# Edge-term gathers moved from the counts into layer 0, the gate ahead of them, uint16 tables, in a graph network kernel

## The reference

```python
h = relu(layernorm(x)); x = x + L0(h)       # gin: (h + segment_sum(h[src], dst)) @ W1, relu, @ W2
h = relu(layernorm(x)); x = x + L1(h)       # attention over the edges
h = relu(layernorm(x)); x = x + L2(h)       # mean over the neighbours
h = relu(layernorm(x)); x = x + L3(h)       # weighted sum over the edges

# L1, per edge and for 8 heads
scores = einsum(q[src], k[tgt]) / sqrt(16) + edges @ We + be
cons   = sigmoid(relu(conservation_scores @ Wc1 + bc1) @ Wc2 + bc2)   # per node: the gate
scores = scores * cons[tgt] + relu(distances @ Wd1 + bd1) @ Wd2 + bd2
weights = softmax of scores over the edges of each tgt
```

## Time and profile before

| | us |
|---|---|
| median of 3 runs | 5038.48 |
| the runs | 5023.93, 5038.48, 5147.51 |
| span of the profiled execution | 5145.3 |
| PE busy in it | 3841.6 (75%) |
| DVE busy | 3822.7 (74%) |
| POOL busy | 2737.6 (53%) |
| ACT busy | 1550.3 (30%) |

### The profile page before, as it was taken

The page is one execution under the profiler, slowest core; times in us unless marked ns, Lnnn a source line. Parts: engine busy times, 40 slices in busy tenths (PEclk is TensorE's granted clock), DMA queues, the critical chain, the costliest instruction groups (busy, mean ns, idle before and its releaser), DMA issues. The chain is left out here.

```text
span 5145.3 us, 93266 instructions
## 1 busy us (share of the span) xinstructions
PE 3841.6 (75%) x26234; PEld 2720.9 (53%) x26235; DVE 3822.7 (74%) x6359; ACT 1550.3 (30%) x3023; POOL 2737.6 (53%) x2300
## 2 busy tenths in 40 slices
PE   4685555550199968888888888888886348889999
PEld 2443222220189835555555555555554248888888
DVE  3516999991299989999999999999996699970000
ACT  2372234560101130122333444445552430020000
POOL 3430199996732227777777777777776232210000
PEclk8799999995599989999999999999997569999999
DMA  9674423346155444454555666666665535568887
GB/s 168 175 234 111 97 100 126 159 175 198 66 193 209 163 140 106 120 146 142 157 165 169 184 184 188 193 196 197 205 204 159 186 113 200 200 213 300 298 297 254
DMA packets 594376, 912.02 MB, mean 177 GB/s; under 512 B 107452, under 2 KB 519442, under 8 KB 575022
## 3 DMA queue, kind: packets, MB, share of 16 engines
q1 hardware_dynamic: 413024, 521.23, 31.2%
q10 hardware_dynamic: 117359, 250.68, 13.4%
q0 software_dynamic: 63872, 138.75, 11.3%
HBM read 608.33 MB, written 311.94 MB: 179 GB/s over the span
## 5 line engine op out<-in xcount | busy, mean ns | idle before, releaser
L1964 POOL DMA_INDIRECT at_qg<-q_d,at_slot x1616 | 1601.2, 991 | 495.8 <-issue 492.2
L986 PE MATMUL bw_ps<-bw_mov,bw_sta 128*128 128x392 bf16 x7056 | 1590.0, 349 | 19.2 <-issue 7.2
L986 PEld LDWEIGHTS bw_ps<-bw_mov,bw_sta 128*128 128x128 bf16 x7056 | 640.4, 102 | 365.0 <-issue 95.6
L2007 PE MATMUL at_psk<-at_kp,at_hot 128*128 x4848 | 611.7, 234 | 286.8 <-DVE at_qg L2085 244.4
L1051 POOL DMA_INDIRECT tv_rows<-ed_d,tv_place x101 | 628.2, 6219 | 339.1 <-DMA edv_d<-tv_rows 211.0
L2007 PEld LDWEIGHTS at_psk<-at_kp,at_hot 128*128 128x128 bf16 x4848 | 439.1, 101 | 624.1 <-issue 418.1
L889 PE MATMUL ba_ps<-ba_mov,ba_sta 128*128 128x392 bf16 x1968 | 380.4, 338 | 352.6 <-DVE ba_sta L830 309.1
L874 DVE TENSOR_SCALAR ba_mov<-iota,key,scale 128x392 bf16<-128x392 f16 x1968 | 592.4, 365 | 2.8 <-PEq L853 2.8
L970 DVE TENSOR_TENSOR bw_sta<-bw_raw,kw 128x1024 bf16<-128x1024 bf16 x882 | 561.2, 689 | 0.0
L830 DVE TENSOR_TENSOR bw_mov<-bw_ps,lo 128x3136 bf16<-128x3136 f16 x294 | 523.4, 1780 | 7.6 <-PE bw_ps L986 5.4
L1566 PE MATMUL at_p3t<-tile,room 128*128 128x256 f32 (+1 forms) x2450 | 524.2, 376 | 4.6 <-ACT room L1150 4.6
(11 more groups left out here) (537 smaller groups left out, 4668.3 us busy)
## 6 DMA issues: line engine op xcount, KB each, us to landing
tile<-adw_d SPq DMA_DIRECT2D x23, 6272.0 KB, 18.7
adw_d<-xall ACTq DMA_DIRECT2D x65, 1568.0 KB
adj_d<-ba_stage ACTq DMA_DIRECT2D x50, 1568.0 KB, 5.1
l0raw<-adj_d SPq DMA_DIRECT2D x50, 1568.0 KB, 6.6
tile<-adj_d SPq DMA_DIRECT2D x50, 1568.0 KB, 6.5
adw_d<-bw_stage ACTq DMA_DIRECT2D x33, 1568.0 KB
at_rel<-rel_d SPq DMA_DIRECT2D x101, 512.0 KB
et_attr<-in_edge_attr SPq DMA_DIRECT2D x48, 1024.0 KB
```

Source lines behind the costliest of these rows:

```text
L986: ins = pe.matmul(self.ps[:, bass.DynSlice(place, WCOL)], self.sta[:, k, u // 2, :, u % 2], self.mov[:, u // 2, :, u % 2], start=False, st ...
L1964: pool.indirect_dma_start(out=qg[:, ring, b, :], out_offset=None, in_=q_d[:, :], in_offset=bass.IndirectOffsetOnAxis(ap=slot[:, ring, b:b ...
L2007: ins = pe.matmul(ps_k[:, at:at + KW], hot[:, par, sum(ROUNDS[:r]) + u, :], kp[:].rearrange("p j k n -> p (j k n)")[:, bass.DynSlice(place ...
```

## The change

Three edits.

1. `terms_by_visits` becomes the class `TermsByVisits` with a ring of two. Its gathers are issued by GpSimd in layer 0, two in each of the 50 steps behind the block's rows and own sums and one behind the last, and its stores by SP, two behind each load of a raw block from the third on. GpSimd's steps of layer 0 are written out where they were a loop. The places of the gathers are copied by VectorE at the start of layer 0.
2. The gate's inputs are loaded by SP ahead of the mask rows, on a semaphore of their own, and GpSimd computes the gate with nothing in front of it in the counts. SP waits for its store before the barrier.
3. The tables of window numbers and window ends are uint16 in memory and on the chip, with one more cast on VectorE for each of the two tables (`firstv_u`).

```diff
-def terms_by_visits(nc, c, ctx):
-
-    ve, pool, sp = nc.vector, nc.gpsimd, nc.sync
-    ring = 4
-    place = ctx.enter_context(nc.sbuf_tensor("tv_place", [P, NG2], I32))
-    rows = ctx.enter_context(nc.sbuf_tensor("tv_rows", [P, ring, 2 * P], F32))
-    s_got, s_kept = ([c.sem(f"tv_{n}{k}") for k in range(ring)] for n in ("got", "kept"))
-    m = c.V(ve.tensor_copy(place[:], c.index[:, :, UK]))
-    wait(pool, m)
-    for g in range(NG2):
-        k, lap = g % ring, g // ring
+class TermsByVisits:
+
+
+    def __init__(self, nc, c, sb):
+        self.nc, self.c, self.ring = nc, c, 2
+        self.place, self.rows = sb("place", [P, NG2], I32), sb("rows", [P, self.ring, 2 * P])
+        self.s_got, self.s_kept = ([c.sem(f"tv_{n}{k}") for k in range(self.ring)] for n in ("got", "kept"))
+
+    def places(self):
+        wait(self.nc.gpsimd, self.c.V(self.nc.vector.tensor_copy(self.place[:], self.c.index[:, :, UK])))
+
+    def gather(self, g):
+        pool, k, lap = self.nc.gpsimd, g % self.ring, g // self.ring
         if lap:
-            pool.wait_ge(s_kept[k], 16 * lap)
-        pool.indirect_dma_start(out=rows[:, k, :], out_offset=None, in_=c.ed_d[:, :], in_offset=bass.IndirectOffsetOnAxis(ap=place[:, g:g + 1], axis=0)).then_inc(s_got[k], 16)
-        sp.wait_ge(s_got[k], 16 * lap + 16)
-        sp.dma_start(c.edv_d[g], rows[:, k, :]).then_inc(s_kept[k], 16)
-    for k in range(ring):
-        sp.wait_ge(s_kept[k], 16 * len(range(k, NG2, ring)))
+            pool.wait_ge(self.s_kept[k], 16 * lap)
+        pool.indirect_dma_start(out=self.rows[:, k, :], out_offset=None, in_=self.c.ed_d[:, :], in_offset=bass.IndirectOffsetOnAxis(ap=self.place[:, g:g + 1], axis=0)).then_inc(self.s_got[k], 16)
+
+    def keep(self, g, k, lap):
+        sp = self.nc.sync
+        sp.wait_ge(self.s_got[k], 16 * lap + 16)
+        sp.dma_start(self.c.edv_d[bass.DynSlice(g, 1), :, :].rearrange("a p n -> (a p) n"), self.rows[:, k, :]).then_inc(self.s_kept[k], 16)
+
+    def kept(self):
+        for k in range(self.ring):
+            self.nc.sync.wait_ge(self.s_kept[k], 16 * len(range(k, NG2, self.ring)))
...
-        c.wreg, c.vend = ctx.enter_context(nc.sbuf_tensor("ba_wreg", [1, NVISV], I32)), ctx.enter_context(nc.sbuf_tensor("ba_vend", [1, NWV // 2], I32))
+        c.wreg, c.vend = ctx.enter_context(nc.sbuf_tensor("ba_wreg", [1, NVISV], U16))
...
+        gate_sb = lambda n, shape: ctx.enter_context(nc.sbuf_tensor(n, shape, F32))
+        c.gate_loaded = load_gate(nc, c, a, gate_sb)
         mask_rows(nc, c)
         load_first_weights(nc, c, a)
-        terms_by_visits(nc, c, ctx)
-        Gate(nc, c, lambda n, shape: ctx.enter_context(nc.sbuf_tensor(n, shape, F32))).run()
+        Gate(nc, c, gate_sb).run()
...
-def load_gate(nc, c, a):
-
-    sp, L, t = nc.sync, c.L, c.gate_in
+def load_gate(nc, c, a, sb):
+
+    CH = 32
+    sp, L = nc.sync, Line(c.sem("gate_here"))
+    t = c.gate_in = [sb("ga_" + n, [P, m]) for n, m in (("v", NB), ("w1", CH), ("b1", CH), ("w2", CH * HEADS), ("b2", HEADS))]
...
-        wait(pool, self.c.first_weights.loaded)
+        wait(pool, self.c.gate_loaded)
...
-        self.c.L.dma(sp.dma_start(self.c.gate_d, self.sums[:].rearrange("p j h -> p (j h)")))
+        self.c.gate_kept = Line(self.c.sem("gate_kept")).dma(sp.dma_start(self.c.gate_d, self.sums[:].rearrange("p j h -> p (j h)")))
+        wait(sp, self.c.gate_kept)
...
+    def sp_with_terms(self, terms):
+
+        def step(i, k, j):
+            if here(i, NBV):
+                self.load(i, k, j * (STEADY // RAW))
+            if here(i - 2, NBV):
+                for t in range(2):
+                    at = 2 * (k - 2) + t
+                    terms.keep(2 * i - 4 + t, at % terms.ring, j * (2 * STEADY // terms.ring) + at // terms.ring)
+        assert 2 * STEADY % terms.ring == 0
+        for i in range(STEADY):
+            step(i, i, 0)
+        with self.nc.sync.Fori(1, NBV // STEADY) as j:
+            for k in range(STEADY):
+                step(STEADY * j + k, k, j)
+        for i in range(NBV // STEADY * STEADY, NBV + 2):
+            step(i, i % STEADY, i // STEADY)
+        for g in range(2 * NBV, NG2):
+            terms.keep(g, g % terms.ring, g // terms.ring)
+        terms.kept()
...
-    def pool(self, first):
+    def pool(self, first, terms=None):
...
+            if terms and here(i, NBV):
+                for g in range(2 * i, min(2 * i + 2, NG2)):
+                    terms.gather(g)
         self.q.high.wait(pool, NB // 7)
-        in_steps(pool, body, max(NBV, NB + self.e.own_lag))
+        steps = max(NBV, NB + self.e.own_lag)
+        if terms:
+            for i in range(steps):
+                body(i, i % STEADY, i // STEADY * (STEADY // RAW))
+            for g in range(2 * NBV, NG2):
+                terms.gather(g)
+        else:
+            in_steps(pool, body, steps)
...
-    layer.sp()
+    terms = TermsByVisits(nc, c, lambda n, shape, dt=F32: sb("tv" + n, shape, dt))
+    layer.sp_with_terms(terms)
+    terms.places()
...
-    layer.pool(bias)
+    layer.pool(bias, terms)
...
-        c.reg_d = nc.dram_tensor("reg_d", (VG * P,), I32, kind="Internal").ap()
-        c.first_d = nc.dram_tensor("first_d", (-(-NW // P) * P,), I32, kind="Internal").ap()
-        c.regv_d = nc.dram_tensor("regv_d", (VGV * P,), I32, kind="Internal").ap()
-        c.firstv_d = nc.dram_tensor("firstv_d", (-(-NWV // P) * P,), I32, kind="Internal").ap()
+        c.reg_d = nc.dram_tensor("reg_d", (VG * P,), U16, kind="Internal").ap()
+        c.first_d = nc.dram_tensor("first_d", (-(-NW // P) * P,), U16, kind="Internal").ap()
+        c.regv_d = nc.dram_tensor("regv_d", (VGV * P,), U16, kind="Internal").ap()
+        c.firstv_d = nc.dram_tensor("firstv_d", (-(-NWV // P) * P,), U16, kind="Internal").ap()
```

More of the change, by code:

```diff
@@ L12 @@
 BF16 = mybir.dt.bfloat16
-I16, I32 = mybir.dt.int16, mybir.dt.int32
+I16, I32, U16 = mybir.dt.int16, mybir.dt.int32, mybir.dt.uint16
 ALU = mybir.AluOpType
@@ L118, in __init__ @@
         self.firsts, self.missing, self.base = t("firsts", P), t("missing", self.columns), t("base", blocks)
-        self.firstv, self.firstv_i, self.low, self.high, self.low_i, self.high_i = (t(n, self.columns, dt) for n, dt in (("firstv", F32), ("firstv_i", I32), ("low", F32), ("high", F32), ("low_i", I32), ("high_i", I32)))
+        self.firstv, self.firstv_u, self.firstv_i, self.low, self.high, self.low_i, self.high_i = (t(n, self.columns, dt) for n, dt in (("firstv", F32), ("firstv_u", U16), ("firstv_i", I32), ("low", F32), ("high", F32), ("low_i", I32), ("high_i", I32)))
         self.where, self.under = (t(n, self.columns * self.groups, BF16) for n in ("where", "under"))
-        self.wt, self.wti, self.cti, self.reg = t("wt", self.groups), t("wti", self.groups, I32), t("cti", self.groups, I32), t("reg", self.groups, I32)
+        self.wt, self.wti, self.cti, self.reg = t("wt", self.groups), t("wti", self.groups, I32), t("cti", self.groups, I32), t("reg", self.groups, U16)
 def index_loads(nc, c, src, dst, edge_weight, sb):
@@ L302, in store_visits @@
             with nc.allow_non_contiguous_dma(reason="short tables"):
-                S.dma(pool.dma_start(first_d.rearrange("(c q) -> q c", q=P), w.firstv_i[:]))
+                S.dma(pool.dma_start(first_d.rearrange("(c q) -> q c", q=P), w.firstv_u[:]))
                 S.dma(pool.dma_start(reg_d.rearrange("(i p) -> p i", p=P), w.reg[:]))
@@ L1060, in build_counts @@
     with ExitStack() as ctx:
[L1061 removed]
+        c.wreg, c.vend = ctx.enter_context(nc.sbuf_tensor("ba_wreg", [1, NVISV], U16)), ctx.enter_context(nc.sbuf_tensor("ba_vend", [1, NWV // 2], U16))
         L.dma(sp.dma_start(c.wreg[:], c.regv_d[0:NVISV].rearrange("(a n) -> a n", a=1)))
@@ L1934, in edge_scores @@
         wait(sp, c.regs_stored)
-        c.wreg, c.vend = tables[0:1, :], tables[32:33, 0:NW]
+        c.wreg, c.vend = tables[0:1, 0:NVIS // 2].bitcast(U16), tables[32:33, 0:NW // 2].bitcast(U16)
         L.dma(sp.dma_start(c.vend, c.first_d[1:NW + 1].rearrange("(a w) -> a w", a=1)))
@@ L2206, in load_firsts @@
             L.dma(sp.dma_start(self.block16[:], c.kreg_d[0:EB].rearrange("(p a) -> p a", a=1)))
-            L.dma(sp.dma_start(self.flag[:], c.mask_d[0][:, 0:1]))
+            return L.dma(sp.dma_start(self.flag[:], c.mask_d[0][:, 0:1]))
     def load_last(self, m_d):
@@ L2741, in place_first_weights @@
     w.biases = [w.b2]
-    CH = 32
-    c.gate_in = [sb("ga_" + n, [P, m]) for n, m in (("v", NB), ("w1", CH), ("b1", CH), ("w2", CH * HEADS), ("b2", HEADS))]
 def load_first_weights(nc, c, a):
@@ L2753, in load_first_weights @@
     L.dma(sp.dma_start(w.b2[:], a["L0_gnn_b2"].rearrange("(a n) -> a n", a=1).to_broadcast([P, D])))
-    c.carries.load_firsts()
-    w.loaded = load_gate(nc, c, a)
+    w.loaded = c.carries.load_firsts()
 class Ctx:
```

2 lines of the change are left out of this document (1 added, 1 removed).

## The result

The changed kernel takes 5518.2 us (median of 4 runs, 5515.28 to 5527.89). The kernel before, timed beside it, takes 5031.2 us (median of 4, 5014.4 to 5147.51). The ratio is 1.0991, with a 95% interval of 1.0956 to 1.1026: slower by 9.9%, where no change was forecast.

A forecast was written before the change was run, and what follows sets the result against it. VectorE was taken to bound the counts, then GpSimd alone (late gathers, gate) until layer 0, where VectorE and TensorE are nearly full. 5145.3 − 126 + 5 + 2.5 + 2 = 5028.8 us span, 5031 us time; range 4920 to 5085.

The forecast's parts named there:

- Part 5: Window number and end tables as uint16: same instructions, half the bytes, one more CAST each; 0, bounded by ±1 us.
- Part 1: Gathers leave the counts: −127 us of late gathers in the profiled execution; the median run was read as having none.
- Part 2: Gate at the start of the counts: 82.2 us still paid, layer 0 opens at 1242 instead of 1368, −126 us.
- the second way: Gate instructions get in during the counts and VectorE stands still, moved by 82 us: −108 us, total 5048, chance 0.19.
- the blocked gathers at 618.89 and 913.11: Gathers held up in the counts, 279 and 244.77 us; taken as sign that the gate is blocked until 1157.
- the 13.55 us row: Layer 0: a GpSimd TENSOR_TENSOR of 13.55 us makes a VectorE one of 3.42 us last 13.56.
- Part 3: Two gathers per step of layer 0: 0.1 us for each of 50 steps, 5 us; range 0 to 22.
- the mild rival: Layer 0: gathers blocked by VectorE's TENSOR_TENSOR, loads as now, 0.8 us a step, 40 us, total 5071; chance 0.07.
- 3 us to spare: Layer 0: raw load behind the gathers' stores is there at 1515.2, its cast starts at 1518.3, so it stays hidden.
- one of four: Layer 0's cycle of raw loads, second gather through merges: 27.0 us for four steps against 30.6, so hidden.
- My upper end: Layer 0: each second gather blocked until the TENSOR_TENSOR ends, 3.4 us later: 0.45 us a step, 22 us.
- Part 4: Ends of layer 0: +2.5 us for first gathers before the bias addition, +2 us for the last gather's store.

The follow-up runs named there:

- e1: The kernel before with a mask (& 0xFFFF) on every value loaded from the int32 tables, nothing else: 5099.98 us, ratio 1.0079.
- e2: The kernel before with the uint16 tables alone, no masks and no moves: 5468.21 us, ratio 1.0805.
- e6: The kernel before with uint16 tables read as int32 pairs, four per load, and split in registers: 5140.23 us, ratio 1.0215.
- e4: The changed kernel with masked int32 tables and its gathers back in the counts, behind the early gate: 5101.95 us, ratio 1.008.
- e8: The kernel before with masked int32 tables and the gate computed in four parts in the index stage, ahead of the counts: 5072.81 us, ratio 1.0088.
- e3: The changed kernel with masked int32 tables instead of uint16, so only the moves of gathers and gate: 5155.73 us, ratio 1.0192.
- e12: e3 with SyncE's stores of the gathered rows one step further back in its queue; on another chip: 6562.79 us, ratio 1.0292.
- e5: The kernel before, int32 tables kept, register loads reading them through a uint16 view with a step of two: 5468.87 us, one run.
- e9: e4 with the 101 gathers issued a second time in layer 0, without stores; on another chip: 6697.27 us, ratio 1.0365.

## Why the prediction was wrong, point by point

- **Part 5, uint16 tables: "0, bounded by ±1 us". This is the step that failed.** Measured alone: +186.8 us in the counts and +200.0 in the rest against e1, which has masks, and 437 us against the median of the kernel before, which like e2 has none (5468.2 − 5031.2). The working counted bytes, elements and the transfers that fill the tables, and never asked who reads them: 246 + 294 loads in TensorE's queue and 50 + 98 in ScalarE's. The trace of before showed those loads at 592 ns, and the forecast had no row for one of another type. So the bound should have come from that row, not from the transfers: 540 loads that might double would have been 320 us. The Trainium skill (DMA: Bandwidth & Descriptors, section "Latency and other measured facts") gives a floor of about 600 ns for `tensor_load`. Loads of eight int32 agree (592 ns); loads of four do not (333 ns in e6, below that floor), and the section says nothing of the type, which makes 1921 ns of the 592 here.
- **Why 1.33 us more a load, 327 us over 246 loads, become some 190 us in the counts.** TensorE's queue had slack: with int32 the group's period was VectorE's. With 1921 ns it is TensorE's, 3.5 us in the group shown, and at the lower granted clock its matmuls are longer too.
- **Part 1, the gather tail: right that it goes; that the median has none is not shown.** No gather is left after the counts, and the runs of after lie within 13 us where those of before span 133. But the 19 runs of the kernel before beside e1 to e4 are spread over 5027 to 5169 with a median of 5090, as tails of many lengths would give (argued, not shown); that the four runs timed beside the change have their median at 5031, near the forecast's base, is in part luck. The kernels in which all gathers were through by 769 us (e1, e2) are ones in which VectorE pauses, and no run of before near 5031 was profiled.
- **Part 2, the gate "paid in full": right in kind, by the second way, and too high.** It was not blocked till 1157. It ran at once, and VectorE nearly stood still for it:

```profile
458.47 3.02 POOL L1223 TENSOR_TENSOR ga_hid<-ga_v,ga_w 128x1568 f32<-128x1568 f32 x1 [137.69 <-DMA ga_b<-in_L_gnn_bc]
...
462.13 16.64 DVE L874 TENSOR_SCALAR ba_mov<-iota,key,scale 128x392 bf16<-128x392 f16 x8
...
543.38 1.01 POOL L1233 TENSOR_TENSOR ga_sums<-ga_sums,ga_b 128x392 f32<-128x392 f32 x1
```

  Eight one-hots take 16.64 us instead of 2.41, and the gate's 82.2 us became 86 (458.47 to 544.39). All moving one-hots together take 662.0 us of VectorE where they took 592.4 before, so about 70 of the 86 us are paid. I had preferred the blocked gathers at 618.89 and 913.11 as the nearer row; a compute instruction of GpSimd behaves like the 13.55 us row. e4 against e1 (1313.53 and 1307.63) shows that moving the gate inside the counts is worth nothing, and e8 that moving it ahead of them gives back 27.5 us.
- **Part 3, layer 0: +5 us, range 0 to 22; measured +61.3** (e3 against e1: +63.8). The mechanism named as the mild rival (gathers held by the TENSOR_TENSOR, SyncE's loads behind their stores, 0.8 us a step, 40 us) is nearest to what came, which is half again as large; whether the lateness of the gathers is all VectorE's doing stays open (e12). The step that failed here is "3 us to spare". It has the second gather landed 3.0 us after its issue, and measured are 5.4 (e3, blocks 10 to 43); the stores and the raw load follow from there, and the raw load lands in 7.2 us instead of 6.6. The raw load then reaches its cast late in 45 of 50 steps (51.3 us of waits in e3), over a cycle of two steps of 17.46 us against 15.3, where I had closed one of four. The ring of two, 8.70 us against 7.66, I didn't close at all. My upper end took a delay of 3.4 us there and came to 0.45 us a step; measured is 1.07 (8.73 − 7.66). The Trainium skill (SBUF — State Buffer, section "SBUF: two separate sides") has the lock between a two-input VectorE instruction and GpSimd; the gather of 4.07 us that ends 0.83 us behind VectorE's 3.42 us agrees.
- **Part 4, the ends of layer 0: +4.5 us.** Not told apart from the rest of layer 0.
- **The sum.** Of the 487 us between the medians, 437.0 are the tables (e2), and 50.0 are left for the moves (5518.2 − 5468.2, a remainder and not a check). By stretches of the profiles, after against e2, the moves are −14.5 us to the opening of layer 0, +62.3 in it and +6.0 in the rest. (The forecast's second way of the gate adds up to 5049, not 5048.)

## What to carry to other kernels

Shrinking a table's element type changes the instructions that read it, not only the bytes that fill it: before such an edit list every reader, registers included, with its duration and what its queue feeds. And a small ring whose refill goes through two transfers has its own period, gather to landing to store to landing; hold that against one step of the loop, as well as the ring that you think is the tight one, and with the landing as long as it is beside the other engines' work.

## What the runs showed of the hardware

- A load into registers took 592 ns for eight int32 (before) and 333 ns for four (e6), and 1921 ns for eight uint16 (after), on TensorE; on ScalarE the shortest of the counts went from 306 to 1092 ns. Whether the uint16 values lay packed (e2) or every second one was skipped (e5) made no difference, 1922 ns in both.
- A gather issued by GpSimd lasted up to 279 us beside a VectorE without pauses, and at most 1.5 us beside one busy 9 parts in 10 (e1).
- In layer 0 of e3 the rows of a step's second gather were there 5.4 us after its start, whether its own row says 0.95 us or 4, so the length of that row doesn't tell when it lands.
- Beside the gate's GpSimd instructions eight one-hots of VectorE took 16.64 us instead of 2.42 (after).
- On two other chips the same kernel took 6446 and 6368 us instead of 5031. Its instructions were not longer (loads of 593 ns, layer 0 of 393.7 us), but TensorE waited 502.2 us for "issue" in front of line 986 in e9, against 33.5 in e1. e9 and e1 are different kernels, but line 986 is the same in both. What holds its queue up there stays open.
